# Routing with its own x buffers, two logit groups and scanned counts, and a gate product that holds the tokens and moves eight columns

## What is computed

```python
xn = _layernorm(x)                                    # 4096 tokens x 256
logits = xt @ gate_w.T + gate_b                       # xt = xn by rows, 8 experts
scores = softmax(logits)
top_w, top_i = top_k(scores, 2)
gate_dense = sum(one_hot(top_i, 8) * top_w[..., None])
...
h = silu(xt @ w1e.T + b1e) * (xt @ w3e.T + b3e)       # each expert e
y = einsum('etd,te->td', h @ w2e.T + b2e, gate_dense)
```

## Time and profile before

| | |
|---|---|
| time, median of 3 runs | 477.03 us (476.67 to 478.61) |
| span of the profiled execution | 476.0 us |
| median less span | 1.0 us |
| routing, to the end of `tile_tok` | 69.1 us |
| busy in the whole span | PE 442.4, PEld 370.7, DVE 370.7, ACT 241.5, POOL 235.9 us |

### The profile page before, as it was taken

The page is one execution under the profiler, slowest core; times in us unless marked ns, Lnnn a source line. Parts: engine busy times, 40 slices in busy tenths (PEclk is TensorE's granted clock), DMA queues, the critical chain, the costliest instruction groups (busy, mean ns, idle before and its releaser), DMA issues.

```text
span 476.0 us, 8336 instructions
## 1 busy us (share of the span) xinstructions
PE 442.4 (93%) x2532; PEld 370.7 (78%) x2532; DVE 370.7 (78%) x700; ACT 241.5 (51%) x396; POOL 235.9 (50%) x222
## 2 busy tenths in 40 slices
PE   0886987988999999999999899999999999999997
PEld 0652464877888888888888778898898989898987
DVE  6967896968788898788776589996868687877863
ACT  4684845488586685958565633332414132423131
POOL 5041787726648685679845286752342516070000
PEclk9999959999999999999999999999999999999999
DMA  6899953335764665343473793735353444432001
GB/s 182 281 349 330 277 88 91 105 140 180 270 232 160 216 209 185 115 152 101 145 189 122 250 323 90 228 104 152 125 148 123 121 150 132 154 108 72 23 23 44
DMA packets 45858, 77.24 MB, mean 162 GB/s; under 512 B 5908, under 2 KB 32252, under 8 KB 45820
## 3 DMA queue, kind: packets, MB, share of 16 engines
q1 hardware_dynamic: 37580, 55.87, 34.0%
q0 software_dynamic: 8240, 20.88, 16.9%
HBM read 48.52 MB, written 28.21 MB: 161 GB/s over the span
## 4 chain that ended last, share of the span: by engine, by line
PE 46%; POOL 17%; DVE 14%; issue 13%; ACT 4%; DMA 4%; SPq 0%; POOLq 0%; DVEq 0%; ACTq 0%
POOL xg L1008 8%; PE ps_w L1545 5%; PE ps_w L1547 5%; PE ps_w L1546 5%; PE ps_w L1611 5%; PE ps_w L1610 5%; PE ps_w L1612 5%; PE ps_g L1085 4%; DMA w_lo<-w_all 2%; POOL den L1020 2%; PE ps_y L1085 2%; POOL den L1019 2%; DVE stats L678 2%; POOL col L1027 2%; POOL firsts L1027 2%
## 5 line engine op out<-in xcount | busy, mean ns | idle before, releaser
L1008 POOL DMA_INDIRECT xg<-xn_rows,tile_tok x71 | 72.7, 1024 | 20.7 <-issue 18.5
L1521 POOL DMA_INDIRECT yg<-expert_rows,rows x64 | 67.8, 1060 | 23.6 <-issue 17.1
L1085 PE MATMUL ps_g<-w_hi,x_hi 128*128 x142 | 56.2, 396 | 1.9 <-DVE x_lo L1240 1.9
L1085 PE MATMUL ps_g<-w_lo,x_hi 128*128 x142 | 56.3, 396 | 0.0
L1085 PE MATMUL ps_g<-w_hi,x_lo 128*128 x142 | 56.1, 395 | 0.0
L1652 ACT ACTIVATE sact<-ps_w,vec_b 128x512 f32<-128x512 f32 x32 | 22.0, 687 | 58.2 <-PE ps_w L1547 58.2
L1545 PE MATMUL ps_w<-col_hi,s_hi 128*128 128x512 f32 x128 | 50.5, 395 | 0.4 <-DVE shid L1763 0.4
L1546 PE MATMUL ps_w<-col_lo,s_hi 128*128 128x512 f32 x128 | 50.2, 392 | 0.0
L1547 PE MATMUL ps_w<-col_hi,s_lo 128*128 128x512 f32 x128 | 50.2, 392 | 0.0
L1085 PE MATMUL ps_y<-w_hi,h_hi 128*128 x142 | 43.1, 304 | 1.3 <-DVE h_lo L1256 1.3
L1249 DVE TENSOR_TENSOR hid<-ps_g,act 128x512 f32<-128x512 f32 (+1 forms) x36 | 23.7, 657 | 24.6 <-ACT act L1161 24.6
(11 more groups left out here) (247 smaller groups left out, 1286.3 us busy)
## 6 DMA issues: line engine op xcount, KB each, us to landing
expert_rows<-y SPq DMA_DIRECT2D x35, 256.0 KB, 2.3
w_lo<-w_all SPq DMA_DIRECT2D x16, 384.0 KB, 10.3
table<-mix_tables SPq DMA_DIRECT2D x8, 768.0 KB, 5.8
xin<-x SPq DMA_DIRECT2D x16, 256.0 KB, 3.5
xn_rows<-xn SPq DMA_DIRECT2D x16, 256.0 KB, 5.2
xn_columns<-xT SPq DMA_DIRECT2D x8, 512.0 KB
col<-xn_columns SPq DMA_DIRECT2D x8, 512.0 KB, 4.7
res<-x SPq DMA_DIRECT2D x16, 256.0 KB, 2.9
```

Of the source, the lines that this page charges most:

```text
L1008: pool.indirect_dma_start(out=xg[b][:, t, :], out_offset=None, in_=xn_d[:, :], in_offset=bass.IndirectOffsetOnAxis(ap=tile_tok[:, first_ti ...
L1085: mm = nc.tensor.matmul(out, x[:, k, :], w[:, ds(e, 1), k, cols].rearrange("p o n -> p (o n)"), start=(k == 0 and n == 0), stop=(last and ...
L1521: pool.indirect_dma_start(out=yg[a.buf(2)][:, k, q, :], out_offset=None, in_=y_d[:, :], in_offset=bass.IndirectOffsetOnAxis(ap=picked[a.bu ...
```

## The change

`gate` is turned round: the token columns are the stationary operand, 128 at a time, and the eight unpadded columns of the gate weights move. That is 4 token blocks by 2 halves of the 256 channels, 8 products of 128x128 by 8 columns in a step, in place of 2 of 128x128 by 512. The logits then stand token by row in `ps_L`, so `logit` and `back` are gone, and `take` adds the bias. There are two groups of four steps.

x is loaded into the memory of `xT`, one buffer for each step, by 16 loads at the head of SyncE's list; the small loads follow them there or go to ScalarE's queue, and the weight parts are issued earlier. The epsilon becomes the bias of the root. The constants on VectorE move behind the first statistics. The counts are scanned on VectorE before TensorE adds them over the partitions, which leaves a shorter chain behind it, and the mask and the shares are made once for all steps. The expert of each tile (`tile_exp`, in rounds 3 to 5 of the hot loop before) is made behind the loop.

```diff
-        NX, NN = 4, 4
+        NN = 4
         MADE, BOTH, HIGH, LOW = 4, 6, 13, 2
         xT = [sb(f"xT{b}", [P, KC, STEP], F32) for b in range(NSTEP)]
-        xin = [sb(f"xin{b}", [P, Q, C], F32) for b in range(NX)]
+        xin = [t[:].rearrange("p k n -> p (k n)").rearrange("p (q c) -> p q c", q=Q) for t in xT]
...
-        SOON = 6
-        ARRIVAL = [4, 5, 6, 7, 0, 1, 2, 3] + list(range(8, E * KC))
+        ARRIVAL = [0, 1, 4, 5, 2, 3] + list(range(6, E * KC))
+        AHEAD, BESIDE = 2, (1, 2, 1, 2, 1, 2, 1, 2)
...
-        GROUPS = [(0, 4), (4, 5), (5, NSTEP)]
-        ROWS = P // 4
-        gw = sb("gw", [P, KC, 2 * P - ROWS], F32)
-        gb = sb("gb", [P, 1], F32)
+        GROUPS = [(0, 4), (4, NSTEP)]
+        gw = sb("gw", [P, KC, E], F32)
...
+            def load_x(i):
                 for b in range(B):
-                    sp.dma_start(xin[a.buf(NX)][:, b * HALF:(b + 1) * HALF, :],
-                                 xv[ds(a.i, 1), :, b, :, :].rearrange("o p h c -> p (o h) c")
-                                 ).then_inc(s_xin[a.buf(NX)], 16)
+                    sp.dma_start(xin[i][:, b * HALF:(b + 1) * HALF, :],
+                                 xv[ds(i, 1), :, b, :, :].rearrange("o p h c -> p (o h) c")).then_inc(s_xin[i], 16)
...
-            load_x(At(0, 0, NSTEP))
-            load_x(At(0, 1, NSTEP))
-            sp.wait_ge(s_gzero, 2)
-            sp.dma_start(gw[:, :, P - ROWS:P - ROWS + E], gate_w).then_inc(s_small, 16)
-            for j in range(4):
-                sp.dma_start(gb[j * ROWS:j * ROWS + E, :], gate_b.rearrange("(n a) -> n a", a=1)).then_inc(s_small, 16)
+            for i in range(NSTEP):
+                load_x(i)
             sp.dma_start(vec_tf[:], first).then_inc(s_small, 16)
             sp.dma_start(vec_td[:], decay).then_inc(s_small, 16)
-            sp.wait_ge(s_gzero, 3)
-            sp.dma_start(w_neg[0:E, :], w_first).then_inc(s_negl, 16)
-            sp.dma_start(w_neg[32:32 + E, :], w_first).then_inc(s_negl, 16)
-            for i in range(2, NX):
-                load_x(At(0, i, NSTEP))
+            arriving = iter(ARRIVAL)
+            for _ in range(AHEAD):
+                load_w(next(arriving))
...
-                if a.i + SOON >= NSTEP:
-                    load_w(ARRIVAL[a.i + SOON - NSTEP])
+                for _ in range(BESIDE[a.i]):
+                    load_w(next(arriving))
...
-                nc.scalar.activation(std[a.buf(2)][:], var[a.buf(2)][:], ACT.Sqrt).then_inc(s_std, 1)
-
-            def logit(g):
-                act.wait_ge(s_L, g + 1)
-                at_least(act, s_LT, g - 1)
-                nc.scalar.activation(gated[g % 2][:], ps_G[g % 2][:], ACT.Identity, bias=gb[:]).then_inc(s_Lg, 1)
+                nc.scalar.activation(std[a.buf(2)][:], mv[a.buf(2)][:, :, 1], ACT.Sqrt, bias=eps[:]).then_inc(s_std, 1)
...
+            act.dma_start(gw[:], gate_w).then_inc(s_small, 16)
+            act.dma_start(gb[:], gate_b.rearrange("(a n) -> a n", a=1).broadcast_to([P, E])).then_inc(s_small, 16)
+            act.wait_ge(s_gzero, 2)
+            act.dma_start(w_neg[0:E, :], w_first).then_inc(s_negl, 16)
+            act.dma_start(w_neg[32:32 + E, :], w_first).then_inc(s_negl, 16)
...
             def gate(a):
                 pe.wait_ge(s_xT, a.i + 1)
                 g, (first, end) = next((g, span) for g, span in enumerate(GROUPS) if a.i < span[1])
-                j = a.i - first
-                if j == 0:
-                    at_least(pe, s_Lg, g - 1)
-                low = P - ROWS - j * ROWS
-                for k in range(KC):
-                    mm = nc.tensor.matmul(ps_G[g % 2][:], gw[:, k, low:low + P], xT[a.i][:, k, :],
-                                          start=(j == 0 and k == 0), stop=(a.i == end - 1 and k == KC - 1))
+                for q in range(Q):
+                    n0 = ((a.i - first) * Q + q) * E
+                    for k in range(KC):
+                        mm = nc.tensor.matmul(ps_L[g][:, n0:n0 + E], xT[a.i][:, k, q * P:(q + 1) * P], gw[:, k, :],
+                                              start=(k == 0), stop=(k == KC - 1))
                 if a.i == end - 1:
                     mm.then_inc(s_L, 1)
...
-            def back(a):
-                for g, (_, end) in enumerate(GROUPS):
-                    if a.i == end - 1:
-                        pe.wait_ge(s_Lg, g + 1)
-                        at_least(pe, s_Lc, g - 1)
-                        for q in range(Q):
-                            mm = nc.tensor.transpose(ps_L[g % 2][:, q, :], gated[g % 2][:, q * P:(q + 1) * P], ident[:])
-                        mm.then_inc(s_LT, 1)
-
-            pe.wait_ge(s_const, 6)
-            pe.wait_ge(s_small, 112)
-            for i in range(NSTEP + 2):
+            pe.wait_ge(s_const, 1)
+            for i in range(NSTEP + 1):
                 if i < NSTEP:
                     turn(At(0, i, NSTEP))
+                if i == 1:
+                    pe.wait_ge(s_small, 64)
                 if 0 < i <= NSTEP:
                     gate(At(0, i - 1, NSTEP))
-                if i > 1:
-                    back(At(0, i - 2, NSTEP))
...
             def less(i):
                 if i in (2, 3):
-                    pe.wait_ge(s_Lc, (3, 2)[i - 2])
+                    pe.wait_ge(s_Lc, i - 1)
...
             pe.wait_ge(s_firsts, 2)
-            pe.wait_ge(s_Lg, len(GROUPS))
             for i in range(2):
                 less(i)
-            pe.wait_ge(s_mask, 2)
-            nc.tensor.matmul(ps_cnt[:, 0, :], before[:], mask[:].rearrange("p e j -> p (e j)"),
-                             start=True, stop=True)
-            nc.tensor.matmul(ps_cnt[:, 1, :], ones[:], mask[:].rearrange("p e j -> p (e j)"),
-                             start=True, stop=True).then_inc(s_cnt, 1)
+            pe.wait_ge(s_upto, 1)
+            nc.tensor.matmul(ps_total, ones[:], upto[:, :, NT - 1], start=True, stop=True).then_inc(s_cnt, 1)
+            nc.tensor.matmul(ps_place, ones[:], upto[:].rearrange("p e j -> p (e j)"), start=True, stop=False)
+            nc.tensor.matmul(ps_place, before[:], mask[:].rearrange("p e j -> p (e j)"), start=False, stop=True
+                             ).then_inc(s_cnt, 1)
...
             def take(g):
                 first, end = GROUPS[g]
-                dve.wait_ge(s_LT, g + 1)
-                nc.vector.tensor_copy(
-                    logits[:, first * Q:end * Q, :].rearrange("p (s q) e -> p s q e", q=Q),
-                    ps_L[g % 2][:].rearrange("p q (s r) -> p s q r", r=ROWS)[:, 0:end - first, :, 0:E]
-                ).then_inc(s_Lc, 1)
+                count = (end - first) * Q
+                dve.wait_ge(s_L, g + 1)
+                dve.wait_ge(s_small, 64)
+                nc.vector.tensor_tensor(
+                    logits[:, first * Q:end * Q, :], ps_L[g][:, 0:count * E].rearrange("p (j e) -> p j e", e=E),
+                    gb[:, None, :].broadcast_to([P, count, E]), ALU.add).then_inc(s_Lc, 1)
 
             measure(At(0, 0, NSTEP))
+            constants()
             for i in range(NSTEP):
                 if i + 1 < NSTEP:
...
                                     ALU.subtract).then_inc(s_firsts, 1)
-            take(1)
             choose(0, 0, EARLY)
-            share(0, 0, EARLY)
             take(len(GROUPS) - 1)
             choose(1, EARLY, NSTEP)
-            share(1, EARLY, NSTEP)
+            own.link(nc.vector.tensor_tensor(mask[:], hot[0].rearrange("p j e -> p e j"),
+                                             hot[1].rearrange("p j e -> p e j"), ALU.add))
+            nc.vector.tensor_tensor_scan(out=upto[:].rearrange("p e j -> p (e j)"),
+                                         data0=keep[:].rearrange("p e j -> p (e j)"),
+                                         data1=mask[:].rearrange("p e j -> p (e j)"), initial=0.0,
+                                         op0=ALU.mult, op1=ALU.add).then_inc(s_upto, 1)
+            share()
 
...
             dve.wait_ge(s_cnt, 1)
-            total = ps_cnt[:, 1, :].rearrange("p (e j) -> p e j", e=E)
-            prefix = ps_cnt[:, 0, :].rearrange("p (e j) -> p e j", e=E)
...
-            own.link(nc.vector.tensor_tensor_scan(out=filled[:].rearrange("p e j -> p (e j)"),
-                                                  data0=keep[:].rearrange("p e j -> p (e j)"),
-                                                  data1=ps_cnt[:, 1, :], initial=0.0,
-                                                  op0=ALU.mult, op1=ALU.add))
-            own.link(nc.vector.tensor_tensor(place[:], filled[:], total, ALU.subtract))
-            own.link(nc.vector.tensor_tensor(place[:], place[:], prefix, ALU.add))
-
-            own.link(nc.vector.tensor_scalar(ntile_i[:], filled[:, :, NT - 1], float(P - 1), float(P), ALU.add,
-                                             ALU.max))
-            own.link(nc.vector.tensor_scalar(ntile_i[:], ntile_i[:], 7, None, ALU.arith_shift_right))
-            own.link(nc.vector.tensor_copy(ntile[:], ntile_i[:]))
```

(80 more changed lines are left out.)

165 lines of the change are left out of this document (67 added, 98 removed).

## The result

The changed kernel takes 487.28 us (median of 4 runs, 486.62 to 491.70) against 477.57 for the kernel before on the same chip: the ratio is 1.0229, 95% interval 1.0190 to 1.0268. The forecast was 486.4, with 468 to 492 around it. The profiled execution has a span of 485.9 us, 9.9 above the 476.0 of before.

The account below looks back on a forecast made before the run. Bound by the routing chain to `tile_tok` (69.14 us), which the experts await. Gate stage 53.7 plus rest 24.84 gives 78.5, +9.4; with span 476.0 and 1.0 to the median, 486.4 us, range 468 to 492.

Parts of the forecast that it names:

- The gate product: TensorE's gate stage: stays at the low clock, loads spaced 0.213 us, step 5.1, last gate product at 53.7, +13.5 us.
- Rival B: TensorE's clock rises after the first gate product, making the change faster: 469.9 us; chance 0.25.
- Rival D: Gate-product loads at the low clock follow each other at 0.131 us, as in f16: 475.9 us, same; chance 0.07.
- C's 0.337: Each gate-product load waits for the pass ahead and stays its whole 0.337 us: 502 us, slower still; chance 0.08.
- The start: First gate product on TensorE at 16.0 us, waiting for the small loads queued behind x.
- The rest: From the last gate product to the end of `tile_tok`: 24.84 us left of 28.99, sum of terms -4.15.
- The hop back: From gate product to VectorE's maximum: one addition, about 0.4 us, in place of ScalarE, transposes and copy: -1.4.
- the choice: `choose` of the last steps on VectorE: four steps in place of three, 3.20 us before, +0.3.
- the way from the mask over scan and count to VectorE's chain: Mask and scan ahead of TensorE's count cost +0.75 us; the weight part no longer awaited gives -1.7.
- the weight products on TensorE: Six weight products stand ahead of the hot loop's products on TensorE and delay the loop: +1.1 us.
- VectorE's shorter chain: VectorE from the counts to the hot loop's first round: 6.69 us before, some 3.5 remain, -3.2.
- One for one: Experts and mixing wait for the token list, so a shift of `tile_tok` carries to the end in full.

## Why the prediction was right

- **The gate product: right, for the reason given.** The spacing was put at 0.213 us, and a step at 5.1; it is 5.01 for 24 loads, 0.209 each, and 0.214 by the run with half the loads. The level was forecast low; it stayed at 1.2 GHz to the end of the stage. That TensorE's busy share is a poor guide is borne out by the run with forty early products: TensorE is busy for 4.00 of 4.00 us from 20 to 24, at a granted clock of 0.50. The hot loop, from which the working took this, has idle time between its rounds (0.46 us in the earlier trace rows) and didn't show it by itself. Rival B needed the level to rise, which 128 moved columns brought about and eight did not.
- **Rival D and the page.** The Trainium skill, page "TensorE: Matmul & The Clock Gate", section "LDWEIGHTS (loading the stationary operand)", gives 1/1.2 ns for each column, an estimate of 0.107 us for 128. The trace agrees only at the high level (0.11 in the run with 128 moved columns); here a load costs 0.209. D's 0.131 of the f16 loads didn't carry over, nor did C's 0.337.
- **The start: 1.2 us off.** It was put at 16.0, by the two small loads. The chain has 17.18, and its releaser is ScalarE's part of the second step's normalising (14.51), then the slow transposes of that step. The small loads land at about 16.5 (the last is issued at 10.69 and takes 5.8 us to landing), and in the run with 31 early products they are what the first gate product waits for, so they would have been next. That this and the smaller spacing cancel, 53.88 against 53.7, is luck. (The row of issues in the earlier trace rows gives how long an issue takes SyncE, as the working reads it, not the time to landing.)
- **The rest: 25.5 against 24.84, right in its terms but one.** The hop back is 0.42 (forecast 0.4), the choice 3.57 (3.5), the way from the mask over scan and count to VectorE's chain 2.42 (2.6), that chain 3.52 (3.5; L751 at 60.29 to L773 at 63.81). The mis-sized term is the weight products on TensorE, +1.1: they run at the low level until 62.3, TensorE is free at 68.47, and the loop takes 15.6 in place of 13.8, +1.8.
- **What the sum hid.** The working booked -3.2 for VectorE's shorter chain, and +0.3, +0.75 and +1.1 against it. The narrow product in the kernel before has none of this, and its rest is 78.91 - 53.3 = 25.6 all the same. There the 3.4 less than before come mostly from the hop back (1.4) and from the shorter wait between mask and count (1.8). Against that kernel the changed one's chain is 3.1 shorter (6.64 and 3.52), but its loop takes 1.9 more (13.67 and 15.59), scan and count 0.6, the choice 0.4. With the wide product the same parts make the rest 29.7, longer than the 28.99 of before, as the loop takes 18.4. That these parts are worth about a microsecond on balance was argued, and the runs don't bear it out.
- **One for one: right here, and up to a point.** Span less `tile_tok` is 406.9 before, 406.5 after, and 406.4 to 407.4 in six of the experiments. In the four traces where the list comes at 63.1 or earlier it is 410 to 413: POOL's late transfers then set the first gather, and TensorE is at the low level behind its longer wait.
- **What would show it:** all signs came but one, the printed clock of 0.50, since no change of it was on record yet.

## What to carry to other kernels

Turning a product round so that few columns move can save multiply work that was not the limit, and leave TensorE at its low clock; here the stage with the same passes and sixteen times the columns, nearly all of them zeros, took 15.7 us less. Price a TensorE stage by durations of instructions whose cost at both levels is known, not by the printed clock, and not by busy time. Before booking a shorter chain as a gain, ask which other engine reaches the meeting point last.

## What the runs showed of the hardware

- The granted clock prints 1.00 until the first change on record: over 50 us of the changed kernel stand at 1.2 GHz under it, as transposes of 0.21 us in place of 0.11 show.
- A high clock was lost within one gate product of 16 loads with eight columns each (17.11 to 19.93), 1.33 us of idle time shortly before, and stayed at 0.50 with TensorE busy for 4.00 of 4.00 us. With 128 columns in each pass it held, behind idle times of 1.69 and 0.82 us.
- A wait of 2.6 us in TensorE's list left the first three of the six weight products behind it slower, 1.67 to 2.07 for two passes (four, 1.71 to 2.08, with the wide gate product), in place of 1.02 to 1.12 where the wait was filled.
- An accumulating transfer that POOL issues mostly takes 1.53 to 2.05 us, or 5.75 to 8.58 where it lasts until after VectorE's hot loop; which of them is held stays open.
